# Selective scan on VectorE: one scan instruction per state over two PSUM banks instead of two instructions over one bank each

## What is computed

```python
dt  = softplus(xf @ W_dt.T + b_dt)                 # [B, T, 256]
dA  = exp(A[None, None] * dt[..., None])           # [B, T, 256, 16]
dBx = dt[..., None] * Bt[:, :, None, :] * xf[..., None]
# h[t] = dA[t] * h[t-1] + dBx[t]  along T, for each channel and state
_, h = jax.lax.associative_scan(comb, (dA, dBx), axis=1)
y   = (h * Ct[:, :, None, :]).sum(-1)
out = y * silu(z) @ W_out.T
```

## Time and profile before

| what | us |
|---|---|
| median of 3 runs | 2667.72 (2667.56 to 2670.8) |
| the profiled execution | 2674.26 |
| its span, first to last instruction | 2672.2 |
| first scan to last scan of phase A | 54.7 to about 1464 |

### The profile page before, as it was taken

How to read it: one execution, slowest core, us unless ns; L and a number is a source line. 1 busy time by engine, 2 the same in 40 slices (tenths; PEclk the granted TensorE clock), 3 DMA queues, 4 the chain that set the end, 5 groups by cost and what they waited for, 6 DMA issues and landing times. The chain is left out here.

```text
span 2672.2 us, 26595 instructions
## 1 busy us (share of the span) xinstructions
PE 2273.9 (85%) x6899; PEld 1108.8 (41%) x6899; DVE 2260.4 (85%) x3630; ACT 1603.4 (60%) x3048; POOL 2068.0 (77%) x1108
## 2 busy tenths in 40 slices
PE   5999999999999999999997207862799999999998
PEld 2444444444444444444443103321455555555544
DVE  2999999999999999999999692223699999999985
ACT  4776777777777777777774203532555555555543
POOL 2889889889889889989988006876688887788872
PEclk8999999999999999999999557985899999999999
DMA  2243333333333333333332202331011111111110
GB/s 77 89 119 114 96 118 115 96 118 113 99 118 108 103 113 107 110 106 113 106 99 87 86 0 54 64 48 28 28 32 32 33 37 39 36 32 32 32 31 18
DMA packets 180610, 199.44 MB, mean 75 GB/s; under 512 B 40062, under 2 KB 170988, under 8 KB 180332
## 3 DMA queue, kind: packets, MB, share of 16 engines
q1 hardware_dynamic: 169196, 189.35, 23.1%
q0 software_dynamic: 11264, 8.40, 2.3%
HBM read 164.44 MB, written 33.25 MB: 74 GB/s over the span
## 5 line engine op out<-in xcount | busy, mean ns | idle before, releaser
L915 POOL TENSOR_TENSOR a_hc<-a_h,a_cs 128x896 f32<-128x896 f32 (+1 forms) x448 | 860.3, 1941 | 55.3 <-DVE a_h L778 54.9
L362 PE MATMUL a_y_bank<-a_hc,a_ident 128*128 128x448 f32 (+1 forms) x1792 | 741.4, 544 | 20.4 <-DVE a_yz L798 19.8
L553 ACT ACTIVATE a_da<-a_dt,a_neg_a 128x448 f32<-128x448 f32 (+1 forms) x896 | 551.8, 631 | 295.7 <-DVE a_h L778 290.7
L778 DVE TENSOR_TENSOR_SCAN a_h<-a_da,a_h,a_dbx 128x448 f32<-128x448 f32 x528 | 583.6, 1136 | 9.5 <-ACT a_da L553 4.4
L362 PEld LDWEIGHTS a_y_bank<-a_hc,a_ident 128*128 128x128 f32 x1792 | 331.6, 190 | 325.3 <-issue 273.0
L1777 PE MATMUL c_p_E<-c_w_ex,c_hid 128*128 128x512 f32 x800 | 375.4, 603 | 17.9 <-DVE c_sc L2032 14.4
L2182 POOL TENSOR_TENSOR c_prod<-c_prob,c_qkv 128x1024 f32<-128x1024 f32 x100 | 280.9, 2834 | 118.6 <-DVE c_prob L2056 118.6
L762 DVE TENSOR_TENSOR a_dbx<-a_dtx,a_b_bank 128x896 f32<-128x896 f32 (+1 forms) x308 | 328.4, 1066 | 15.7 <-PE a_b_bank L355 15.5
L903 POOL TENSOR_TENSOR a_dbp<-a_dtx,a_bs 128x896 f32<-128x896 f32 (+1 forms) x140 | 271.6, 1940 | 0.0
L778 DVE TENSOR_TENSOR_SCAN a_h<-a_da,a_h,a_dbp 128x448 f32<-128x448 f32 x240 | 263.7, 1132 | 0.0
L2173 POOL TENSOR_TENSOR c_prod<-c_qkv 128x1024 f32<-128x1024 f32 x100 | 232.0, 2352 | 21.6 <-ACT c_qkv L1845 21.5
(11 more groups left out here) (309 smaller groups left out, 3712.5 us busy)
## 6 DMA issues: line engine op xcount, KB each, us to landing
a_cs<-c_rows SPq DMA_DIRECT2D x96, 896.0 KB, 5.3
a_bs<-c_rows SPq DMA_DIRECT2D x24, 1120.0 KB, 5.6
a_cs<-c_rows SPq DMA_DIRECT2D x16, 900.0 KB, 4.4
c_x<-h_rows SPq DMA_DIRECT2D x100, 64.0 KB, 2.2
heads<-c_ot SPq DMA_DIRECT2D x25, 256.0 KB, 2.0
c_dealt<-heads SPq DMA_DIRECT2D x200, 32.0 KB, 1.9
rolled<-c_res SPq DMA_DIRECT2D x25, 256.0 KB, 2.4
h_rows<-a_th SPq DMA_DIRECT2D x24, 224.0 KB
```

The lines of the kernel that those rows point to most:

```text
L362: pe.matmul(y_bank[:, d, 0:g.w], ident[:], hc[:, (g.i * NS + n) % HC_RING, d, 0:g.w], start=(n == 0), stop=(n == NS - 1)).then_inc(s_sum, 1)
L553: act.activation(da[:, k % DA_RING, 0:g.w], dt[g.slot][:, d, 0:g.w], ACT.Exp, scale=neg_a[:, d * NS + n:d * NS + n + 1]).then_inc(s_da, 1)
L778: dve.tensor_tensor_scan(h[:, n, d, 0:g.w], da[:, (g.i * 2 * NS + k) % DA_RING, 0:g.w], x, state, ALU.mult, ALU.add).then_inc(s_scan, 1)
L915: pool.tensor_tensor(hc[:, (q.i * NS + n) % HC_RING, :, 0:q.w], h[:, n, :, 0:q.w], cs[:, n % C_RING, 0:q.w].unsqueeze(1).to_broadcast([P, ...
```

## The change

- **Scan.** A state has one scan of 897 columns (901 in an image's first chunk): half 0, one column between, half 1. The tiles `dbx`, `dbp` and `h` get that column. In it the decay is a constant 0 and the addend is the second half's state from the chunk before, so the scan arrives at half 1 with that state. 16 scans a turn stand in the place of 32.
- **Decays.** `da` is three neighbouring banks. State n even takes banks 0 and 1, n odd takes banks 1 and 2, so that the two halves meet at a bank's border; bank 1 is used by every state. `early(n)` writes the half in the outer bank once scan n - 2 is done and copies the carried column (128 x 1); `late(n)` writes the half in bank 1 once scan n - 1 is done. A scan waits for all three.
- **Order.** VectorE has one scan where two stood, with the products and the other work between them in a new order; the lists of ScalarE, TensorE and GpSimd are rearranged too, with `WORK_ORDER` (which work bank a result uses). On ScalarE `small_exp` stands between `late(7)` and `early(8)`. On TensorE both `dt` projections stand ahead of `b_and_c`.
- Two memsets of one column are added ahead of the loop, one for each border of banks.

The core of the diff:

```diff
-            for d in range(2):
-                k = g.i * 2 * NS + 2 * n + d
-                need(act, s_scan, k + 1 - DA_RING)
-                act.activation(da[:, k % DA_RING, 0:g.w], dt[g.slot][:, d, 0:g.w], ACT.Exp,
-                               scale=neg_a[:, d * NS + n:d * NS + n + 1]).then_inc(s_da, 1)
+        def decay(g, n, d):
+            first = (n % 2 + 1) * 512 - g.w if d == 0 else (n % 2 + 1) * 512 + 1
+            act.activation(da[:, first:first + g.w], dt[g.slot][:, d, 0:g.w], ACT.Exp,
+                           scale=neg_a[:, d * NS + n:d * NS + n + 1]).then_inc(s_da, 1)
+        def outer_bank(g, n):
...
+            K = g.i * NS + n
+            need(act, s_scan, K - 1)
+            decay(g, n, n % 2)
...
+            last = zeros[:, 0:1] if g.first else h[:, n, 2 * g.w_before:2 * g.w_before + 1]
+            act.copy(carried(g, n)[:, g.w:g.w + 1], last).then_inc(s_da, 1)
+
+        def middle_bank(g, n):
+            need(act, s_scan, g.i * NS + n)
+            decay(g, n, 1 - n % 2)
...
-        def scan(g, n, d):
-            k = 2 * n + d
-            dve.wait_ge(s_da, g.i * 2 * NS + k + 1)
+        def scan(g, n):
+            K = g.i * NS + n
+            dve.wait_ge(s_da, 3 * K + 3)
...
-            dve.tensor_tensor_scan(h[:, n, d, 0:g.w], da[:, (g.i * 2 * NS + k) % DA_RING, 0:g.w],
-                                   x, state, ALU.mult, ALU.add).then_inc(s_scan, 1)
+            first = (n % 2 + 1) * 512 - g.w
+            dve.tensor_tensor_scan(h[:, n, 0:2 * g.w + 1], da[:, first:first + 2 * g.w + 1],
+                                   carried(g, n)[:, 0:2 * g.w + 1], state, ALU.mult, ALU.add).then_inc(s_scan, 1)
```

More of the change, by code:

```diff
@@ L179, in nth_on_pool, with both, carried @@
         return g.i * N_POOL + POOL_STATES.index(n)
+    def both(tile, g):
+        return tile[:, 0:2 * (g.w + 1)].rearrange("p (d c) -> p d c", d=2)[:, :, 0:g.w]
+    def carried(g, n):
+        if n in POOL_STATES:
+            return dbp[:, nth_on_pool(g, n) % DBP_RING]
+        return dbx[:, nth_on_dve(g, n) % DBX_RING]
     def scans_of(states, k):
-        return 2 * (k // len(states) * NS + states[k % len(states)] + 1) if k >= 0 else 0
+        return k // len(states) * NS + states[k % len(states)] + 1 if k >= 0 else 0
     wtok = sb("wtok", [PV, D])
@@ L567, in scalar, with early, late, next_early @@
         for q, p, r, f in turns:
-            def decays(n):
+            def early(n):
                 if q:
-                    decay(q, n)
-            def next_decays():
+                    outer_bank(q, n)
+            def late(n):
+                if q:
+                    middle_bank(q, n)
+            def next_early():
                 if p:
-                    decay(p, 0)
+                    outer_bank(p, 0)
+            def next_late():
+                if p:
+                    middle_bank(p, 0)
             def silus():
@@ L699, in keep_norm @@
                     store(r, "trn", tn, s_tn_out, r.outs_before)
[L701 to L704, removed]
+            early(1)
+            late(1)
+            early(2)
+            late(2)
+            early(3)
+            late(3)
+            early(4)
+            late(4)
             silus()
-            decays(5)
-            decays(6)
+            early(5)
+            late(5)
             biased(0)
-            decays(7)
+            tail()
+            early(6)
+            late(6)
+            early(7)
             biased(1)
-            decays(8)
+            late(7)
             small_exp()
+            early(8)
+            late(8)
+            early(9)
             keep_b_and_c()
+            late(9)
+            keep_rows()
             one_more()
-            decays(9)
-            keep_rows()
             middle_b()
-            decays(10)
+            early(10)
+            late(10)
+            early(11)
             square_out()
             low_b()
-            decays(11)
-            log_of_sum()
[L723 to L727, removed]
+            late(11)
+            early(12)
+            scale_out()
+            late(12)
+            keep_token()
+            log_of_sum()
+            early(13)
             square()
+            late(13)
+            early(14)
             keep_logit()
-            decays(14)
+            late(14)
             scales()
-            decays(15)
+            early(15)
+            late(15)
+            next_early()
+            next_late()
+            affine()
             keep_norm()
-            next_decays()
-            affine()
     def vector(dve):
@@ L742, in vector @@
         dve.memset(eps_cols[:, 1:2], EPS * EPS / (1 + EPS))
+        for bank in (1, 2):
+            dve.memset(da[:, 512 * bank:512 * bank + 1], 0.0)
         dve.memset(zeros[:], 0.0).then_inc(s_const, 1)
@@ L948, in gpsimd @@
             weigh(0)
+            product(6)
             weigh(1)
-            product(6)
             weigh(2)
@@ L954, in gpsimd @@
             weigh(4)
+            product(12)
             weigh(5)
-            product(12)
             weigh(6)
```

135 lines of the change are left out of this document (61 added, 74 removed).

## The result

| | before | after |
|---|---|---|
| median of four runs each | 2668.01 us (2667.56 to 2670.8) | 2730.82 us (2726.43 to 2731.79) |
| the profiled execution | 2674.26 | 2726.43 |
| its span | 2672.2 | 2724.5 |

The change makes the kernel slower by 62.8 us: ratio 1.0234, 95% interval 1.0221 to 1.0246. In the profiled executions the difference is only 52. Phase A alone grows by 62.6 us: its last gate starts at 1468.14 before and at 1530.71 after.

The account below looks back on a forecast made before the run. VectorE's queue was taken to bound phase A. 24 chunks at +1.9 us (45), 4 first chunks (8) and the last scanning turn (-2) gave about +51 on the median of 2667.7: 2719 us, range 2685 to 2757.

Parts of the forecast that it names:

- What bounds phase A: Phase A: VectorE's queue bounds it, busy 49.83 of 50.62 us a turn; phases B and C stay at 1188 us.
- The merged scan: VectorE's scans: one of 897 columns costs 1.98 us instead of 2.10, saving 0.12 each, 1.8 us a turn.
- The rival that a scan over a border of banks is no cheaper: VectorE's wide scan costs 2.10 us or a bit more: +1.9 us a turn, 2770 us; chance 0.06.
- The shared bank: Scans right behind another wait for the late decay: 2.77 us from scan to scan against 1.98, 0.79 lost each.
- Scan 5: State 5's scan waits for ScalarE, whose block `silus` ends 6.41 us behind the gate: 1.74 us lost.
- The sign it gave: VectorE idle before scans, put down to ScalarE's decays: 3.5 to 5 us a turn, largest about 1.7 behind two products.
- idle at the products: VectorE idle at products, for TensorE, would mean that TensorE's rows are the bound; no size given.
- Scan 8 and the small ones: State 8's scan loses 0.59 us behind `small_exp`; states 10 and 15 lose 0.2 each to ScalarE's operations.
- What costs nothing: ScalarE's copies (3 us) stand beside scans apart from the counted waits; TensorE's 47.6 and GpSimd's 45.2 us fit in 52.5.
- The turn and the sum: Phase A: 47.5 us of queue work plus 5.0 of waits make a turn of 52.5; all turns together add 51.
- ramp-up: Start of phase A: put at 0, its ScalarE and TensorE work only reordered, a microsecond either way.
- The last scanning turn: End of phase A's scans: no block `silus` there, so 2 us are taken off the sum.

Follow-up runs that it names:

- Run 2: The kernel after with each state's scan cut in two again and the halves of `h` 451 columns apart, not 449: 2790.35 us, ratio 1.046.
- Run 1: The kernel after with four decay banks, so neighbouring states share none, and both halves of y summed into one bank: 2682.34 us, ratio 1.0064.
- run 8: The kernel after without the two table loads of the block `silus`, which applies the identity instead of silu: 2716.73 us, ratio 1.0178.
- run 3: The kernel before, with its two scans a state, ring and early decays, in the order of work of the kernel after: 2693.26 us, ratio 1.0098.
- run 5: The kernel after with states 3, 5, 6 and 8 scanned in two halves, outer bank first, in 24 of 28 chunks: 2705.41 us, ratio 1.015.
- run 6: The kernel after with GpSimd's weighing of state 8 held back until `lost` is done: 2771.94 us, ratio 1.0397.
- run 12: The kernel after with two columns between the halves instead of one, so 450 columns apart and not 449: 2730.07 us, ratio 1.0241.
- run 4: The kernel after with odd states' decays in SBUF, `dbp` cut to two buffers, GpSimd's products 12 and 15 later: 3016.19 us, ratio 1.1321.
- run 9: The kernel before with 5.3 of 16 states a turn scanned by one instruction, halves 450 columns apart: 2666.38 us, ratio 0.9998.
- run 11: The kernel before with 5.3 of 16 states a turn merged, but one column between the halves, so 449 apart: 2682.84 us, ratio 1.0062.

## Why the prediction was right, and which terms were off

The forecast of 2719 us held the sign and the mechanism; the time came out 12 us longer, inside its range. That the profiled execution, forecast at 2725, took 2726.43 is chance: it lay below the median of its kernel and that of before above. By its steps:

- **What bounds phase A.** Held. The medians differ by 62.8 us and phase A in the profiled executions by 62.6, so nothing is left for phases B and C.
- **The merged scan.** It lasts 2.08 (forecast 2.07) and costs 2.00 from start to start (forecast 1.98): it saves 0.10 and not 0.12. Run 2 shows the same 0.10 by undoing it. 16 x 0.02 is 0.3 a turn, 9 us in all. The rival that a scan over a border of banks is no cheaper is refuted.
- **The shared bank.** Held: 2.79 from scan to scan, forecast 2.77. Run 1 takes the waits away and gives back 48 us, 45 by the ratios.
- **Scan 5.** Held: the block ends 6.41 behind the gate, exactly as worked out, and 1.63 are lost where 1.74 were forecast. The rows alone cost 1.2 (run 8), where the prediction had 1.1. The sign it gave was put too simply: in the trace most of this wait stands at the two products, as idle for TensorE, and only 0.20 at the scan. So the idle put down to ScalarE's decays is 0.71 + 0.20 + 0.71 + 0.25 = 1.9 us a turn and not 3.5 to 5, and the largest is 0.71. The prediction took idle at the products as a sign that the rows are the bound; they are the larger part of this one wait, and ScalarE ends it.
- **Scan 8 and the small ones.** Too large. Scan 8 loses 0.32, not 0.59: from the late decay of state 7 to scan 8 are 3.70 us (972.99 to 976.69) where the step has 3.95, since it added durations, and neighbours on ScalarE overlap; the copy costs 0.08 from start to start and not 0.19. At state 10 0.04 are lost and at 15 nothing, where 0.2 each were put.
- **What costs nothing.** This is the step that failed, for TensorE and GpSimd. GpSimd's order was followed for its amount of work and not for what its work does to VectorE. `lost` has both inputs in SBUF. Before, GpSimd sat idle waiting for it (2.61 us in the turn shown); now it weighs beside it, and `lost` costs 1.38 instead of 0.98, 0.4 a turn and about 11 us. Runs 2, 3, 5, 6 and 12 show it come, go and move: where GpSimd waits in run 6, `lost` is back at 1.06. The same step misses a second, smaller term: product 1 starts 0.2 late. Its row on TensorE (950.82) stands behind sums that wait for GpSimd's weighing, slower by the distance of 449 columns; with 450 it starts on time (run 12).
- **The turn and the sum.** 16 x 2.00 + 15.8 of other work, 0.4 more for `lost`, waits of 2 x 0.79 + 1.63 + 0.32 + 0.04, four own products 0.74 and 0.2 at product 1 give 52.7, and the trace has 52.71. A first chunk's turn went from 49.70 to 51.77 (from 50.05 to 51.76 in the last image): +2.07, forecast 2.1. At the first gate, behind one scanning turn, the difference is 2.9, where the sum has 2.1: ramp-up is not quite 0. The last scanning turn was to be even (+1.9 - 2) and cost +4.2 from gate to gate. Without `lost`, `steps` and the work of the next chunk on VectorE, its scans 11, 14 and 15 stand bare, each with 0.7 of idle for the late decay, and `normed_out` waits 1.39 for ScalarE.

In a regular turn the misses are +0.3 (pitch), +0.4 (`lost`) and +0.2 (product 1) against -0.27, -0.36 and -0.11 (scan 8, states 10 and 15, scan 5): +0.2 of the 2.09, some 4 us over all regular turns. The last scanning turn adds 4 us, the one before it 1, the stretch to the first gate 1 and the turns at the ends of images 1. With what the forecast's sum rounded off, these make the 12. That a regular turn came out within 0.2 is in part luck: 0.9 of misses on one side were met by 0.7 on the other.

As for contention, the Trainium skill (SBUF — State Buffer, Who interferes with whom) has the rule that I left out: a VectorE instruction with two inputs in SBUF contends with a GpSimd instruction that reads SBUF, as an exclusive lock in which issue order decides who waits. The traces agree: 2.85 or 1.07 for the same `lost` (run 12), 3.09 against 2.08 for a scan with both streams in SBUF (run 4). By that rule the term could have been asked for in advance, since the new order puts GpSimd's weighing beside `lost`.

## What to carry to other kernels

Merging two instructions saves their fixed part only where everything that the merged one needs is early; look at the ring first, since a buffer shared by neighbours turns a hidden hand-over into a wait in every place without work between. Merge in some places and leave the others: 4.7 merged scans a turn, in the old order and without a shared bank, beat 0 by 5.8 us; 16, with a shared bank and a new order, lost 63. And when an order changes, ask of each VectorE operation with both inputs in SBUF what GpSimd does beside it, whether or not GpSimd bounds anything.

## What the runs showed of the hardware

- One VectorE scan may read over the border of two PSUM banks, and the rows show no price for it: 2.07 to 2.08 us for 897 or 898 columns against 2.19 for two of 448 back to back.
- GpSimd's product of 128x896 with halves 450 columns apart takes 1934 ns, with halves 449 apart 2095 (runs 9 and 11). In the kernel after it is 2144, with 450 columns 1985 (run 12), with 451 columns 1948 (run 2, where the scans are cut in two). So it is not simply an odd distance; the cause stays open.
- A VectorE operation of 1.07 us with both inputs in SBUF took up to 3.69 us beside GpSimd (run 3), and a scan of 2.08 took 3.09 on average with both streams in SBUF (run 4). Where `lost` came 0.5 before the end of a weighing it took 0.4 longer (after), where it came 1.8 before 1.6 longer (run 2). Whether it or GpSimd waits can change from turn to turn in one execution (run 12).
